# Early work of a fused attention kernel: preparation, projections and attention in one block, weights turned on demand, quantised weights' transposes among the fills

## What is computed

```python
def _L0_xattn_ref(q, k, v, ...):          # 16 heads of 16
    qh, kh, vh = heads(q @ Wq.T + bq), heads(k @ Wk.T + bk), heads(v @ Wv.T + bv)
    scores = softmax(einsum('bhqd,bhkd->bhqk', qh, kh) / 4)
    col_sum = sum(scores, axis=2)
    mask = one at the top 460 of 512 columns of col_sum, zero elsewhere
    return (scores * mask) @ vh -> concat @ Wo.T + bo
def _L0_ffn_ref(x, w_gate, w_up, w_down): # x and weights in blocks of 16 to fp4 and back
    return fp4_linear(silu(fp4_linear(x, w_gate)) * fp4_linear(x, w_up), w_down)
def _L1_xattn_ref(ctx, x, ...):           # linear attention: (k.T @ v) per head, then q @ it
    return layer_norm(q @ kv * scale + x) * gamma + beta
def _L1_ffn_ref(x, weight, bias):         # int8: rows of x and of the weight to integers
    return (x_q @ w_q.T) * x_scale * w_scale.T + bias

x = x + tanh(g_xattn[0]) * _L0_xattn_ref(_layernorm(x), ctx, ctx, ...)
x = x + tanh(g_ffn[0]) * _L0_ffn_ref(_layernorm(x), ...)
x = x + tanh(g_xattn[1]) * _L1_xattn_ref(ctx, _layernorm(x), ...)
x = x + tanh(g_ffn[1]) * _L1_ffn_ref(_layernorm(x), ...)
```

## Time and profile before

| what | value |
|---|---|
| time, median of 3 runs | 1296.64 us (1295.99 to 1300.9) |
| the profiled execution | 1297.85 us, its span 1296.1 us |
| PE busy in the span | 1045.4 us (81%) |
| DVE busy | 1041.7 us (80%) |
| ACT busy | 884.1 us (68%) |
| POOL busy | 111.7 us (9%) |
| mean granted clock of TensorE | 0.954 of full speed |

### The profile page before, as it was taken

How to read it: one execution, slowest core, us unless ns; L and a number is a source line. 1 busy time by engine, 2 the same in 40 slices (tenths; PEclk the granted TensorE clock), 3 DMA queues, 4 the chain that set the end, 5 groups by cost and what they waited for, 6 DMA issues and landing times.

```text
span 1296.1 us, 17705 instructions
## 1 busy us (share of the span) xinstructions
PE 1045.4 (81%) x5688; PEld 507.7 (39%) x5688; DVE 1041.7 (80%) x2086; ACT 884.1 (68%) x1935; POOL 111.7 (9%) x111
## 2 busy tenths in 40 slices
PE   2868999987777776776776775888999999999985
PEld 2545665541111111111111111235666767676663
DVE  5675668788888888888888884456999999999965
ACT  2315656559999999999999993574545554555532
POOL 4140110010000000000000000001111111111111
PEclk8878999998999999999999997788999999999987
DMA  7324643222222221220222201101111111110000
GB/s 221 114 73 106 164 146 107 74 82 38 40 42 42 43 42 36 37 41 20 38 42 42 43 18 41 47 9 38 49 33 33 47 45 41 33 57 25 17 17 33
DMA packets 77888, 71.78 MB, mean 55 GB/s; under 512 B 13738, under 2 KB 71396, under 8 KB 77796
## 3 DMA queue, kind: packets, MB, share of 16 engines
q1 hardware_dynamic: 77796, 70.65, 20.9%
HBM read 42.83 MB, written 27.28 MB: 54 GB/s over the span
## 4 chain that ended last, share of the span: by engine, by line
PE 42%; ACT 36%; DVE 11%; issue 8%; SPq 1%; DMA 1%; POOL 0%; ACTq 0%; DVEq 0%
ACT ea L1124 20%; ACT prob L1132 14%; PE ps_a L1339 11%; PE ps_b L1298 6%; PE ps_c L1298 4%; PE ps_v L1298 2%; PE ps_a L1319 2%; PE ps_b L629 2%; PE ps_b L619 2%; PE ps_b L563 1%; PE ps_a L1348 1%; DVE nmax L1025 1%; PE ps_c L981 1%; PE ps_v L997 1%; PE ps_b L951 1%
## 5 line engine op out<-in xcount | busy, mean ns | idle before, releaser
L1124 ACT ACTIVATE ea<-ps_a,nmax 128x512 f32<-128x512 f32 x512 | 363.2, 750 | 71.3 <-DVE nmax L1025 71.3
L1025 DVE TENSOR_REDUCE nmax<-ps_a 128x2 f32<-128x1024 f32 x256 | 313.0, 1223 | 60.0 <-PE ps_a L951 58.8
L1132 ACT ACTIVATE prob<-ps_b 128x1024 f32<-128x1024 f32 x256 | 279.5, 1092 | 46.7 <-PE ps_b L951 46.7
L951 PE MATMUL ps_b<-q_st,k_st 52*128 52x512 f16 x512 | 102.1, 395 | 142.0 <-ACT prob L1132 141.8
L951 PEld LDWEIGHTS ps_b<-q_st,k_st 52*128 52x128 f16 x512 | 25.0, 93 | 369.1 <-ACT prob L1132 337.2
L1339 PE MATMUL ps_a<-wgu,xT 128*128 128x352 f32 x512 | 164.3, 465 | 2.5 <-ACT xT L1463 2.3
L997 PE MATMUL ps_v<-prob,v_in 128*16 128x512 f32 x1024 | 137.8, 610 | 11.6 <-DVE att L1092 11.4
L981 PE MATMUL ps_c<-ea,rz 128*32 128x512 f32 x1024 | 138.1, 612 | 0.0
L1124 ACT ACTIVATION_READ_ACCUMULATOR ea<-ps_a,nmax 128x1 f32 x512 | 137.0, 268 | 0.0
L1339 PEld LDWEIGHTS ps_a<-wgu,xT 128*128 128x128 f32 x512 | 94.2, 191 | 50.0 <-issue 4.6
L1476 ACT ACTIVATE ea<-ps_a 128x352 f32<-128x352 f32 x128 | 59.4, 464 | 76.2 <-PE ps_a L1339 76.2
(11 more groups left out here) (269 smaller groups left out, 1634.2 us busy)
## 6 DMA issues: line engine op xcount, KB each, us to landing
q_scr<-q_p SPq DMA_DIRECT2D x24, 256.0 KB, 2.5
k_scr<-k_p SPq DMA_DIRECT2D x24, 256.0 KB, 2.9
q_st<-q_scr SPq DMA_DIRECT2D x32, 192.0 KB, 4.7
k_st<-k_scr SPq DMA_DIRECT2D x32, 192.0 KB, 5.1
x_in<-in_x SPq DMA_DIRECT2D x8, 512.0 KB, 5.1
c_in<-in_ctx SPq DMA_DIRECT2D x8, 512.0 KB, 4.8
v_scr<-v_s SPq DMA_DIRECT2D x8, 512.0 KB, 2.9
v_in<-v_scr SPq DMA_DIRECT2D x16, 256.0 KB, 3.2
```

The source lines that it names most:

```text
L951: return e.matmul(bank, left[b][o:o + rows, r, t * P:t * P + P], right[b][o:o + rows, r], start=True, stop=True)
L1025: e.tensor_reduce(nmax[u % 2][:, t].rearrange("p (h r) -> p r h", h=2)[:, r], ps_a[:, z % 2 * 2:z % 2 * 2 + 2], AX_X, ALU.max, negate=True ...
L1124: e.activation(ea[c % RING][:, g % 4], ps_a[:, g % 4], ACT.Exp, bias=nmax[u % 2][:, t, n:n + 1], accum_out=tot[u % 2][:, t, n:n + 1]).then ...
L1132: e.activation(at.prob[g % RING][:, 2 * (z % 2):2 * (z % 2) + 2], ps_b[:, :, :], ACT.Exp).then_inc(s_prob, 1)
```

## The change

`prepare` is no block any more: its parts become functions of each engine, called between the fills. Each weight has its own semaphore and is turned when the fills need it. A batch's slots are put in a new order, context first. `scales` and `round` move to later fills. The transposes of the quantised weights are no stage any more but eleven fills (negative entries of `SEQ`), one after every third slot from slot 56. 24 slots instead of 32 stand ahead of the steps; the other 130 entries are spread over steps 0 to 40. Two pairs of POOL's memsets of `q_st` and `k_st` (`ones(2)`, `ones(3)`) now wait until all quantised weights are turned, because the memory is shared with them.

```diff
+CT0, GRAM, K0, V0, XT0, Q0, Q1 = 0, 3, 5, 8, 10, 13, 15
+X1, RB, KV, MM, ROW = 2, 4, 7, 12, 14
...
+    SEQ = []
+    for n in range(FILLS * B + ROW + 1):
+        SEQ.append(n)
+        if n >= 56 and n % 3 == 2 and (n - 56) // 3 < fp4.GROUPS:
+            SEQ.append(~((n - 56) // 3))
...
+        def first():
+            tokens_of(0)
+            weight(WK)
...
+            weight(WV)
+            inputs_of(0)
+            weight(WQ)
...
+            weight(WK1)
+            weight(WV1)
+            tokens_of(1)
...
+            inputs_of(1)
+
+        def second():
+            weight(WO)
+            e.dma_start(w8n[:, :, :], chunks(a["L1_ffn_weight"])).then_inc(s_w8, 16)
...
+        def turn(n):
+            k = TURNS.index(n)
+            e.wait_ge(s_w[n], 48 if n in (WK1, WV1) else 16)
...
+        def round_w8():
+            e.wait_ge(s_w8, 16)
+            e.wait_ge(w.s_set, CONST)
...
         def batch(b):
             if b + 2 < B:
+                load_c(b + 2)
+            store_k(b)
+            store_v(b)
+            if b + 2 < B:
                 load_x(b + 2)
-            store_q(b)
-            store_k(b)
-            if b + 2 < B:
-                load_c(b + 2)
             if b:
                 store_m(b - 1)
-            store_v(b)
+            store_q(b)
...
-    AHEAD = 2
+    AHEAD = 24
...
+            first()
             fp4.load(e)
-            for b in range(AHEAD):
-                project(b)
+            second()
+            project(0)
             load_heads(0)
             load_heads(1)
+            project(1)
             project(2)
+            project(3)
+            project(4)
             load_heads(2)
-            project(3)
             load_values(0)
-            project(4)
             place_shifts(0)
...
+            fp4.split(e, 0)
+            row_parts(0)
+            fp4.split(e, 1)
+            fp4.split(e, 2)
+            row_parts(1)
+            row_parts(2)
+            row_parts(3)
+            e.wait_ge(fp4.s_turned, fp4.GROUPS)
+            for n in range(2, 4):
+                ones(n)
...
+            for n in range(AHEAD):
                 fill(n)
-            fp4.transposes(e)
-            fp4.done(e)
+                if n == CT0 + 1:
+                    weight(WK)
+                    weight(WV)
+                    bias_columns()
+                if n == GRAM:
+                    weight(WQ)
+                if n == V0 + 1:
+                    weight(WK1)
+                    weight(WV1)
+                if n == Q1:
+                    weight(WO)
+                    turn_w8()
+            e.wait_ge(w.s_w8, 1)
...
+            def fill_and_round(s):
+
+                fill(s)
+                if s == 14:
                     fp4.scales(e)
-                if n == 12:
+                if s == 22:
                     fp4.round(e, 0)
-                if n == pj.fills + 3:
+                if s == 33:
                     fp4.round(e, 1)
-                if n == pj.fills + 9:
+                if s == 44:
                     fp4.round(e, 2)
-            fp4.copies(e, 1)
+
+            for n in range(AHEAD):
+                fill_and_round(n)
+                if n == GRAM:
+                    bias_columns()
+                    bias_operand()
+                if n == V0 + 1:
+                    round_w8()
+                if n == Q1:
+                    gated()
+                if n == Q1 + 2:
+                    scale_w8()
```

More of the change, by code:

```diff
@@ L128, in tokens, with __init__, operands @@
     return x.rearrange("(c p) d -> p c d", p=P)
+class Tiles:
+    def __init__(self, m, nc, ctx, a, w):
+        HALF = H // 4
+        with ExitStack() as early:
+            self.early = Mem(nc, early, ctx)
+            self.prepare = prepare_tiles(self.early)
+        self.ring = m.sb("ea", [P, 4, 4, T])
+        self.q_st, self.k_st = [], []
+        def operands(n):
+            self.q_st.append(m.sb(f"q_st{n}", [P, HALF, T], F16))
+            self.k_st.append(m.sb(f"k_st{n}", [P, HALF, T], F16))
+        for n in range(2):
+            operands(n)
+        with ExitStack() as early:
+            self.fp4 = Fp4Weights(Mem(nc, early, ctx), a, w)
+        for n in range(2, 4):
+            operands(n)
+        self.v_in, self.att = m.two("v_in", [P, TT, P]), m.two("att", [P, T])
 def build(nc, a, out):
@@ L135, in build @@
         w = Weights(m)
+        tiles = Tiles(m, nc, ctx, a, w)
+        fp4 = tiles.fp4
+        at = attend(m, w, scr, tiles)
         with ExitStack() as early:
[L138 to L145, removed]
+            me = Mem(nc, early, ctx)
+            ey = Early(me)
+            fp4.with_scales(me)
+            pr = prepare(me, a, w, ey, tiles.prepare, [at.ps_a[:, n] for n in range(4)])
+            pj = project(me, a, w, ey, scr, [at.ps_b[:, 0], at.ps_b[:, 1], at.ps_v[:, :]], fp4)
@@ L189, in _ @@
[L189 to L202, removed]
-                            pattern=[[-DK, P // DK], [0, DK]], channel_multiplier=1).then_inc(s_const, 1)
-            e.wait_ge(s_const, 2)
-            e.affine_select(out=bv, in_=bv, compare_op=ALU.is_ge, fill=0.0, base=DK - 1,
-                            pattern=[[DK, P // DK], [0, DK]], channel_multiplier=-1).then_inc(s_const, 1)
@@ L400, in transposes @@
                                       self.dn[:, oc, (c + j) * P:(c + j) * P + k], ident[:, :])
[L401 to L415 removed]
+        ins.then_inc(self.s_turned, 1)
@@ L837, in attend @@
     at = Stage()
-    ring = m.sb("ea", [P, RING, 4, T])
+    ring, q_st, k_st, v_in, att = tiles.ring, tiles.q_st, tiles.k_st, tiles.v_in, tiles.att
     ea = [ring[:, n] for n in range(RING)]
-    q_st, k_st = ([m.sb(f"{x}{n}", [P, NP, T], F16) for n in range(BUFS)] for x in ("q_st", "k_st"))
-    v_in = m.two("v_in", [P, TT, P])
     rz = m.sb("rz", [P, TT, 2, 4, 32])
@@ L1774, in feed, with run @@
     return fd
[L1777 removed]
+def run(nc, whole, w, pr, fp4, pj, at, fd):
     at.stored, at.opened = pj.stored, pj.banks_left
[L1782 removed]
+    AHEAD = 24
     OPEN = 41
```

664 lines of the change are left out of this document (364 added, 300 removed).

## The result

The changed kernel takes 1303.31 us, the median of 20 runs (1300.32 to 1308.54), the kernel before 1299.93 us in as many (1295.99 to 1302.78). The ratio is 1.0033, with a 95% interval from 1.0021 to 1.0044. The change makes the kernel slower, by a third of a per cent. The forecast was 1273 us, and the time measured is outside its range.

A forecast was written before the change was run, and what follows sets the result against it. PE bounds the overlapped stretch, ACT the attention behind it. First maximum at 60.4, plus 179.2 of PE work and 10 of stalls, gives 249.6 against 272.9: 23.3 us off 1296.6, 1273 us; range 1260 to 1291.

The forecast's parts named there:

- The start: Before attention, 24 fills instead of two whole batches: first maximum on DVE moves from 106.4 to about 60.5 us.
- Rival D: Loads of `w8n` and quantised weights hold the 24 fills; start at 70 rather than 60 us; 1283 us, chance 0.12.
- PE's work: Overlapped stretch: 16 us of batch 1's second half and weight transposes added to 167.1, giving 183.1 us.
- The stalls: Overlapped stretch: PE loses 3 us at `round(1)`, 4 at `round(2)`, 3 to memsets, 10 us in all.
- The mark of 249.6: End of the overlapped stretch, X1 behind the last batch: forecast at 249.6 us instead of 272.9, 23.3 earlier.
- Other things I cost at nothing.: Third unit's loads, the last waits before step 42 and the ACT table load: counted as costing nothing.
- Rounds and splits: DVE's rounds and POOL's splits: `round(0)` 5.5 us and KV's wait 3.4 before the first maximum; later pairs cost 3 and 4.
- PE has X1, GRAM, RB and one or two steps, 7 to 8 us, which hides the rounding itself: Behind `round(1)`, after CT1 of batch 2: PE's queued work covers DVE's rounding; 3 us lost through `split(1)`.
- The turns: Overlapped stretch: eleven groups of transposes of the quantised weights add 5.1 us of PE work.
- The 3 us for the memsets: Four POOL memsets of `q_st` and `k_st`, 1.8 us each, moved into the overlapped stretch: 3 us in all.
- Rival C: Overlapped stretch: DVE sets the pace, its work growing from 118.3 to 155.8, length to 220; 1304 us, slower, chance 0.06.
- 1.5 us for this, once: Before attention, batch 1's X1 to K1: some 1.5 us more on 10.6 us since PE has stood still.

The follow-up runs named there:

- Kernel 11: Changed kernel with early layer norm, rounds and splits in pieces, and DVE doing each group's last fill behind the next step's maximum: 1271.10 us, ratio 0.9796.
- kernel 1: Changed kernel with ACT's two layer-norm writes moved from the V slots to the KV product's slot: 1288.59 us, ratio 0.9935.
- kernel 5: Kernel before the change, with the next batch's two layer-norm writes moved from slots 8 and 13 to 14 and 15: 1294.96 us, ratio 0.9978.
- kernel 8: Changed kernel with the layer norm at the KV product's slot and without DVE's rounds and GpSimd's splits: 1271.70 us, ratio 0.9792.
- kernel 10: Kernel 8 without the turns of the quantised weights, transposes and copies both: 1260.14 us, ratio 0.9706.
- kernels 9 and 6: Both: changed kernel with early layer norm and each round cut into four; 6 measured 1283.35 us; 9, with the splits' instructions also cut in four, 1276.88 us.
- Kernel 2: Changed kernel with the last four slots of batches 1 to 7 reordered to ROW, Q0, Q1, MM: 1301.98 us, ratio 1.0043.

## Why the prediction was wrong

**The start was right, step by step.** The load of `w8n`, the rounding, the scales, X1 behind Q1's low part, `round(0)`, and the KV product held for 3.23 us (3.4 was taken): 58.72 against 60.5. (The terms written out give 60.2, not 60.4, and KV's first product, 0.60 us, has none; both are too small to matter.) Rival D is out.

**PE's work was right, at the clock that the kernel before had in this stretch** (0.98). I had 183.1 us for the stretch. Kernel 11, with the same 898 instructions, shows 180.23 at 0.99.

**The stalls were wrong**, and with them the sum. Ten microseconds were allowed. From the first maximum to the mark PE was idle for 33.9 us, 23.9 more than that, and its work took 186.8 us where 179.2 were counted. The whole stretch of the changed kernel holds 39.7 us of idle PE, and its 898 instructions took 190.9 us where kernel 11 needs 180.2, 10.7 us more, about the ratio of the granted clocks (0.93 and 0.99). The mark of 249.6 was 279.4.

Three terms carry this. The first is the step that failed, the other two were mis-sized:

1. **"Other things I cost at nothing."** The list under this sentence has loads, waits and a table load, but not the order of the fills within a batch. The order excerpts that I read were of DVE and PE; ACT's queue I didn't walk, since ACT was 41% idle in the stretch. The layer norm stands directly ahead of XT, on a queue whose head waits for a maximum. That cost 12.7 us (kernel 1), and the forecast had 0. It costs so much only together with the late maxima and short cover of the new order: in kernel 5 the same place cost nothing.
2. **Rounds and splits.** The 5.5 us of `round(0)` with 3.9 of V beside it, 3.4 for KV, then 3 and 4 for the two later pairs: the round and its KV wait put 4.8 us on the start (60.4 less 3.9, against 51.7 without them), so 11.8 in all. Measured 18.6 (kernel 8 against 1). "PE has X1, GRAM, RB and one or two steps, 7 to 8 us, which hides the rounding itself" was probably the fault: those steps' maxima are in the queue of the blocked engine. So PE comes to an operand or a bank that DVE has yet to hand over while it still has work behind that.
3. **The turns.** 5.1 us of PE, 11.2 measured (kernel 10 against 8). By the two stretches 7.1 us is PE's work and 4.9 us idle time. Each turn also puts a copy into ACT's or DVE's queue, which may be where the idle time comes from.

The excess over the forecast, by ratios, is 1.0033 less 1273/1296.64 = 0.9818, or 0.0215, 27.9 us. The three terms give 12.7 + 6.8 + 6.1 = 25.6 of it. They are single differences with 3 to 4 us of uncertainty each, so that the sum comes so near is in part luck. The 3 us for the memsets weren't measured by themselves.

**Rival C gave 1304, the time measured, but for another reason.** It had DVE set the pace, the stretch growing in proportion to its work (155.8 forecast, 156.49 measured, and 230.5 us of length against its 220). Kernel 11 has 150.89 us of DVE work in 195.30 us, 77% busy, where the kernel before had 71% and the changed kernel 68%. DVE could take the work in; the order and the pieces in which it came were the matter. I had argued against C that "PE waits under 1 us for DVE in any place". That was true before, and no evidence for a queue with other things in it. In the changed kernel 17.5 us of PE's waits name DVE directly, and 22.0 name ACT, the longest of them with DVE behind it.

## What to carry to other kernels

When a change reorders work in in-order queues, walk each new neighbour pair on every engine: for each instruction, what stands directly ahead of it and what that one waits for. An average of idle time doesn't show that ACT's operand for PE is behind an exponential, behind a maximum, behind a round. Put what closes a loop between engines (here the maximum) at the head of its group, operands a few slots ahead of their readers, and long side work in pieces shorter than the cover; here these three edits turned a loss of 0.3% into a gain of 2.0%.

## What the runs showed of the hardware

- **A stall of PE costs twice.** In the stretch of the changed kernel the same 898 PE instructions took 190.9 us at a mean granted clock of 0.93, and 180.2 us at 0.99 in kernel 11, where PE stood idle for 15.1 and not 39.7 us. Time multiplied by clock is about 178 us in both. X1 took 3.05 us behind the wait of 4.35 us shown above, and 2.0 us in the earlier trace rows. I had allowed 1.5 us for this, once.
- **GpSimd in four pieces loses little.** By the timelines the first pass of `split(0)` took 3.86 us as four instructions and 3.42 as one, the second 3.23 and 2.81 (kernels 9 and 6); beside DVE's work the second pass of `split(1)` took 4.68. DVE gets in between.
- **A change of the wait's name is not a gain.** Kernel 2 took 7 us of waits for `q_p` away and the time didn't move.
